# Cross-attention on one core: whole output tiles in sequence, the range check between the norms, and the choice loaded ahead of the wait for the stores

## The reference

```python
Q = (input_Q @ W_Q).reshape(b, -1, N_HEADS, D_K).transpose(0, 2, 1, 3)
K = (input_K @ W_K).reshape(b, -1, N_HEADS, D_K).transpose(0, 2, 1, 3)
V = (input_V @ W_V).reshape(b, -1, N_HEADS, D_V).transpose(0, 2, 1, 3)
scores = jnp.einsum('bhqd,bhkd->bhqk', Q, K) / np.sqrt(D_K)
attn = jax.nn.softmax(scores, axis=-1)
context = jnp.einsum('bhqk,bhkd->bhqd', attn, V)
context = context.transpose(0, 2, 1, 3).reshape(b, -1, N_HEADS * D_V)
out = context @ W_O + input_Q
mu = jnp.mean(out, axis=-1, keepdims=True)
var = jnp.var(out, axis=-1, keepdims=True)
return (out - mu) / jnp.sqrt(var + 1e-05)
```

## Time and profile before

| | before |
|---|---|
| median of 3 runs | 1643.43 us (1643.36 to 1644.0) |
| profiled execution, its own time | 1643.83 us |
| its span, first to last instruction | 1642.1 us |
| mean granted TensorE clock | 0.998 |
| TensorE matmul busy | 1626.4 us (99%) |
| VectorE busy | 1237.4 us (75%) |
| ScalarE busy | 964.8 us (59%) |
| GpSimd busy | 63.3 us (4%) |
| DMA, mean over the span | 6 GB/s |

### The profile page before, as it was taken

The page is one execution under the profiler, slowest core; times in us unless marked ns, Lnnn a source line. Parts: engine busy times, 40 slices in busy tenths (PEclk is TensorE's granted clock), DMA queues, the critical chain, the costliest instruction groups (busy, mean ns, idle before and its releaser), DMA issues.

```text
span 1642.1 us, 39623 instructions
## 1 busy us (share of the span) xinstructions
PE 1626.4 (99%) x17542; PEld 642.3 (39%) x17542; DVE 1237.4 (75%) x1184; ACT 964.8 (59%) x1079; POOL 63.3 (4%) x38
## 2 busy tenths in 40 slices
PE   9999999999999999999999999999999999999997
PEld 3443334333343334433344333443334433344334
DVE  5778787787877878777787777878777787777876
ACT  5556655555656556565655666556565565655652
POOL 0001010000100001000000100001000010000100
PEclk9999999999999999999999999999999999999999
DMA  4000000000000000000000000000000000000000
GB/s 158 2 2 1 2 2 2 1 1 2 1 2 2 1 2 2 2 2 1 2 2 2 2 1 2 2 1 2 1 1 2 2 2 1 2 2 2 1 1 15
DMA packets 6367, 9.53 MB, mean 6 GB/s; under 512 B 432, under 2 KB 4016, under 8 KB 6192
## 3 DMA queue, kind: packets, MB, share of 16 engines
q1 hardware_dynamic: 5760, 6.36, 1.2%
q10 hardware_dynamic: 432, 0.59, 0.1%
HBM read 6.42 MB, written 0.52 MB: 4 GB/s over the span
## 4 chain that ended last, share of the span: by engine, by line
PE 98%; DVE 1%; DMA 0%; ACT 0%; issue 0%; SPq 0%; ACTq 0%
PE o_ps L345 43%; PE s_ps L328 43%; PE w_ps L392 7%; PE w_ps L375 5%; PE s_ps L415 0%; DMA ctx_all<-in_ctxT 0%; PE o_ps L415 0%; PE w_ps L415 0%; ACT probs L509 0%; DVE sums L607 0%; DVE k_all L595 0%; DVE y L683 0%; DVE limits L619 0%; DVE y L666 0%; PE o_ps L392 0%
## 5 line engine op out<-in xcount | busy, mean ns | idle before, releaser
L607 DVE TENSOR_TENSOR sums<-sums,probs 128x1024 f32<-128x1024 f32 (+1 forms) x800 | 999.9, 1250 | 364.4 <-ACT probs L509 357.5
L509 ACT ACTIVATE probs<-s_ps 128x1024 f32<-128x1024 f32 x816 | 836.9, 1026 | 644.3 <-PE s_ps L328 626.6
L328 PE MATMUL s_ps<-q_sb,k_all 64*64 64x512 f32 x6528 | 846.8, 589 | 0.8 <-DVE q_sb L595 0.6
L345 PE MATMUL o_ps<-probs,v_all 64*64 64x512 f32 x6528 | 846.5, 589 | 0.0
L328 PEld LDWEIGHTS s_ps<-q_sb,k_all 64*64 64x64 f32 x6528 | 248.9, 133 | 452.2 <-issue 447.3
L345 PEld LDWEIGHTS o_ps<-probs,v_all 64*64 64x64 f32 x6528 | 244.7, 133 | 392.5 <-issue 388.0
L375 PEld LDWEIGHTS w_ps<-wv_sb,ctx_all 64*64 64x64 f32 x3232 | 96.3, 133 | 59.7 <-issue 52.0
L375 PE MATMUL w_ps<-wv_sb,ctx_all 64*64 64x128 f32 x3232 | 107.1, 270 | 0.4 <-DVE k_all L595 0.4
L392 PE MATMUL w_ps<-ctx_all,wk_sb 64*64 64x512 f32 (+1 forms) x832 | 106.9, 584 | 0.6 <-DMA ctx_all<-in_ctxT 0.6
L303 POOL TENSOR_TENSOR o_b<-o_a,o_b 128x512 f32<-128x512 f32 x15 | 31.5, 2098 | 1290.0 <-ACT o_a L540 1290.0
L595 DVE TENSOR_TENSOR k_all<-k_all,w_ps 128x512 f32<-128x512 f32 (+1 forms) x104 | 69.6, 669 | 6.6 <-ACT k_all L518 6.6
(11 more groups left out here) (52 smaller groups left out, 115.0 us busy)
## 6 DMA issues: line engine op xcount, KB each, us to landing
ctx_all<-in_ctxT SPq DMA_DIRECT2D x12, 256.0 KB, 5.6
xT_sb<-in_xT ACTq DMA_DIRECT2D x2, 256.0 KB, 4.5
x_sb<-in_x SPq DMA_DIRECT2D x1, 512.0 KB, 10.4
wo_sb<-in_wo SPq DMA_DIRECT2D x1, 512.0 KB, 11.4
out<-y SPq DMA_DIRECT2D x4, 128.0 KB, 2.0
wq_sb<-in_wq SPq DMA_DIRECT2D x1, 448.0 KB, 7.0
wk_sb<-in_wk SPq DMA_DIRECT2D x1, 448.0 KB, 7.7
wv_sb<-in_wv SPq DMA_DIRECT2D x1, 448.0 KB, 8.4
```

The source lines that it names most:

```text
L328: last = nc.tensor.matmul(s_ps[part(half), u % 2, head * QH:(head + 1) * QH], k_all[part(head), c * P + half * DH:c * P + (half + 1) * DH] ...
L345: last = nc.tensor.matmul(o_ps[part(head), rows, :], v_all[part(rows), c, part(head)], probs[part(rows), u % RING, head * QH:(head + 1) * QH],
L509: nc.scalar.activation(probs[:, u % RING, :], s_ps[:, u % 2, :], ACT.Exp, scale=SCALE).then_inc(probs_ready, 1)
L607: nc.vector.tensor_tensor(out=sums[0:rows, t % 2, :], in0=sums[0:rows, t % 2, :], in1=probs[0:rows, u % RING, :], op=ALU.add).then_inc(sum ...
```

## The change

TensorE projects tiles 4, 5, 6 and 7 whole, one after another. The wait for the last normalisation moves ahead of tile 4's eighth pair, and the counting matmul moves ahead of tile 7; it now waits for two tiles taken, where it waited for all eight. VectorE does the norm of tiles 0 to 3, then the range check with the choice, then the norm of tiles 4 to 7. SyncE loads the choice between the second and the third store. TensorE, ScalarE and VectorE load it where they did, at the end of their streams.

```diff
-        def if_general(eng, program):
+        def load_choice(eng):
             eng.wait_ge(choice_ready, 1)
-            chosen = eng.value_load(use_general[0:1, 0:1], min_val=0, max_val=1)
+            return eng.value_load(use_general[0:1, 0:1], min_val=0, max_val=1)
+
+        def if_general(eng, chosen, program):
             with eng.If(chosen > 0):
                 program()
...
-            def store(turn):
-                for n in range(QT // 2):
+            def store(turn, groups):
+                for n in groups:
                     sp.wait_ge(ln_done, QT * turn + 2 * n + 2)
                     sp.dma_start(out_t[:, 2 * n:2 * n + 2, :], y[:, 2 * n:2 * n + 2, :]).then_inc(stored, 16)
...
-            store(0)
+            store(0, (0, 1))
+            chosen = load_choice(sp)
+            store(0, (2, 3))
             sp.wait_ge(stored, 16 * (QT // 2))
-            if_general(sp, general_and_store)
+            if_general(sp, chosen, general_and_store)
...
             pe.wait_ge(o_added, PASSES)
-            for t in (4, 5):
-                project_output(t, range(PAIRS - 1))
+            project_output(4, range(PAIRS - 1))
+            pe.wait_ge(last_norm_done, 1)
+            project_output(4, [PAIRS - 1]).then_inc(y_done, 1)
+            project_output(5, range(PAIRS)).then_inc(y_done, 1)
 
             pe.wait_ge(work_ready, COUNT["d", PASSES - 1, 0])
-            for t in (6, 7):
-                project_output(t, range(PAIRS - 1))
-            pe.wait_ge(last_norm_done, 1)
-            for t in range(QT // 2, QT):
-                project_output(t, [PAIRS - 1]).then_inc(y_done, 1)
-
-
-            pe.wait_ge(y_taken, QT)
+            project_output(6, range(PAIRS)).then_inc(y_done, 1)
+
+            pe.wait_ge(y_taken, 2)
             pe.wait_ge(exact_ready, 1)
             nc.tensor.matmul(s_ps[0:1, 0, 0:1], exact[:, :], ones[:, 0:1], start=True, stop=True).then_inc(exact_counted, 1)
+            project_output(7, range(PAIRS)).then_inc(y_done, 1)
...
-            if_general(pe, general)
+            if_general(pe, load_choice(pe), general)
...
             dve.wait_ge(xres_loaded, 32)
-            layer_norm(0)
-
+            layer_norm(0, (0, 1))
 
             for n in range(2):
                 find_limit(last, n)
...
             nc.vector.tensor_scalar(out=use_general[:, :], in0=s_ps[0:1, 0, 0:1], scalar1=P - 0.5, scalar2=None,
                                     op0=ALU.is_lt).then_inc(choice_ready, 1)
 
+            layer_norm(0, (2, 3))
+
```

More of the change, by code:

```diff
@@ L280, in general_and_store @@
                 general()
-                store(1)
+                store(1, range(QT // 2))
                 sp.wait_ge(stored, 2 * 16 * (QT // 2))
             out_t = out.rearrange("(t p) d -> p t d", p=P)
-            store(0)
+            store(0, (0, 1))
+            chosen = load_choice(sp)
+            store(0, (2, 3))
             sp.wait_ge(stored, 16 * (QT // 2))
-            if_general(sp, general_and_store)
+            if_general(sp, chosen, general_and_store)
         @block.gpsimd
@@ L584, in _ @@
             roots(0)
-            if_general(act, general_and_roots)
+            if_general(act, load_choice(act), general_and_roots)
         @block.vector
@@ L656, in _, with layer_norm @@
                                     op=ALU.mult).then_inc(last_norm_done, 1)
-            def layer_norm(turn):
+            def layer_norm(turn, groups):
                 STEPS = 5
-                for n in range(QT // 2):
+                for n in groups:
                     before = STEPS * (QT // 2 * turn + n)
@@ L770, in general_and_norm @@
                 dve.wait_ge(stored, 16 * (QT // 2))
-                layer_norm(1)
-            if_general(dve, general_and_norm)
+                layer_norm(1, range(QT // 2))
+            if_general(dve, load_choice(dve), general_and_norm)
 def kernel(**inputs):
```

## The result

The changed kernel takes 1638.80 us (median of 9 runs, 1637.69 to 1639.22) against 1643.36 us (median of 9, 1642.35 to 1644.0): ratio 0.9973, 95% interval 0.9964 to 0.9982. It is faster, by 4.56 us, where 5.97 was forecast; the time lies 0.1 above the upper end of the range and 1.3 above the predicted one.

A forecast was written before the change was run, and what follows sets the result against it. TensorE's 4.18 us branch after the late choice bounds the kernel; afterwards SyncE's stores end it at 1635.9, plus 0.23: span 1636.13, 5.97 us saved. From the median 1643.43 that gives 1637.5 us, range 1636.7 to 1638.7.

The forecast's parts named there:

- What bounds the kernel before: At the kernel's end: choice at 1636.63, plus loading 0.87, TensorE's branch 4.18, DRAIN and barrier about 0.4 us.
- (1): TensorE doing tiles 4 to 7 in sequence: 1.79 us a tile, tile 6 whole at 1628.37, moved wait costs nothing.
- (2): Range check of 2.00 us fills VectorE's 3.58 us hole; TensorE's wait for it has 0.38 us slack, no cost.
- (3): Choice known at 1628.74 against 1636.63, 7.89 us earlier; VectorE idles from 1627.85 to 1628.74 for it.
- (4): Norms of tiles 4 to 7 on VectorE: last row of y ready at 1633.44, 0.76 us earlier.
- (5): SyncE's choice load hidden between stores 2 and 3, else 0.8 us; last store lands after 1.8 us; SyncE ends at 1635.9.
- rival B: TensorE's branch ends the kernel, its fetch falling among stores 3 and 4; 1638.4 us at 1.3 times its length; chance 0.09.
- (6): TensorE's branch stays and costs 4.18 us again but no longer starts last; through DRAIN at 1635.55, before SyncE.
- A: The stores end the kernel: 1637.5 us, own range 1636.7 to 1638.4; chance 0.82.
- C: Choice later than forecast, by a range check over 2.38 us or unhidden SyncE load; 1638.3 at 0.8 late; chance 0.04.
- D: SyncE's branch stalls behind the stores as TensorE's does; 1641.2 us, no measurable difference; chance 0.04.
- E: Slower: TensorE's branch needs its blocks one after another behind store packets; four stalls of 4.18 give 1649.7 us; chance 0.01.

The follow-up runs named there:

- the experiment: The changed kernel with SyncE's load of the choice put back behind the wait for the stores: 1639.42 us (ratio 0.9980).
- the rerun: The changed kernel itself measured once more, with no edit: 1638.49 us (ratio 0.9975), last store landing after 3.5 us.

## Why the prediction was right and where it was wrong

**What bounds the kernel before**: right, and shown by the kernel without TensorE's branch. Its span ended at 1638.5 and not at the 1638.0 that the text gave for a kernel with a short branch: VectorE's DRAIN at 1638.2 comes after SyncE's, and the 0.23 to the end of the span behind that.

**(1) and (2), TensorE's order and the check in the hole**: right. Tile 6 ends 12.71 us after the projection's start, as worked out, and TensorE never waits for the check: it ends at 1627.04, the counting matmul starts at 1627.55.

**(3), the choice**: 7.89 earlier forecast, 7.96 measured. VectorE waited 0.67 for it.

**(4), the last norms**: right within 0.2. The last store is issued at 17.60 after the start, forecast 17.79; the choice's end and the next norm's first addition overlap.

**(5), SyncE's queue**: the load is hidden, and its price of 0.8 is right (the experiment gave 0.9). The landing is the step that failed. I took 1.8 us, "the row of the store that, like this one, has a TensorE that is done". The rows had that wrong way round: what set the 2.6 us store apart was the packet of q8 in its time, which the earlier trace rows held and which the text used, under rival B, to argue that the stores would lengthen TensorE's branch. It was the other way: the branch's packets lengthen the store, here from 1.8 to 3.0 us. The text also moved TensorE's branch ahead by over 6 us without asking what else its fetch would meet, and it never placed the packets of ScalarE's and VectorE's jumps. The packet of TensorE that does the harm is the second one, behind the jump's end. In the kernel before it moved at 1642.4, after the end of the span, where the earlier trace rows did not look (the DMA view of 1642.1:1643.1):

```profile
q8 instruction: 1, 0.02, 6.0%
```

**(6), TensorE's branch**: right that it stays and is covered. It ran 1628.8 to 1632.2, the earlier of the two cases, and took 3.42 us where 4.18 was assumed; being covered, the difference moved nothing.

**The sum**: from the projection's start, 20.47 forecast and 21.35 measured in the first profile. The parts: issue 0.2 sooner, landing 1.2 later (3.0 for 1.8), SyncE's way from the landing to the end 0.13 shorter (0.75 for 0.88). In the rerun, whose profiled execution (1638.47) lies at its median, the landing is 1.7 later, and -0.2 + 1.7 - 0.1 = 1.4 from the projection's start. The medians miss 1637.46 by 1.3 (1638.80) and 1.0 (1638.49). The landing is thus the only part that is long enough for the miss; closer than that the account does not go, because the projection's start itself moves by up to 1.0 us from profile to profile.

**The range** allowed 0.8 for the landing, the worst row seen, which had one packet in its time. Here there were three. **The rivals**: A was right in kind, the stores end it. B, C, D and E did not come.

**How one packet does it** can be read in part. In the profile with q8 alone the packet ends 1.5 us after the issue, and the trickle begins there. In the rerun it starts at 0.9 and takes 1.5 us, so it ends at 2.4, and there the second part of the trickle begins. How many of the store's packets start more than 1.5 us after its issue is in the DMA view of the 2 us from there on, here with ScalarE's and VectorE's jumps held back (1634.05:1636.05), with TensorE's held back (1634.31:1636.31), and in the rerun (1633.82:1635.82):

```profile
q1 hardware_dynamic: 16, 0.01, 2.4%
```
```profile
q1 hardware_dynamic: 17, 0.01, 1.4%
```
```profile
q1 hardware_dynamic: 34, 0.02, 4.2%
```

In the kernel with no jumps on three engines there are none. 272 packets over 16 DMA engines are 17 each, so this looks like one engine that serves its share only behind the instruction packet, and two of them in the rerun. The other stores of the fourteen profiles say the same. The second always has a q8 packet in its data and lands after 2.3 to 2.8 us; the first always has one of q14 and lands after 2.0 to 2.3. In all, 17 stores meet a q8 packet alone while their data moves, and each lands 1.1 to 1.2 us after that packet's end. Stores whose packets all ended within 0.7 us of the issue, or started 1.46 us or more after it, land after 1.8 to 1.9. So what counts is less how many packets there are than when they end. No view shows the single engines, so that a packet and a share wait on the same one is inferred, not shown. How the packets lie in executions that were not profiled is open too.

## What to carry to other kernels

When a step is moved ahead, ask what its engines do next and where that now falls: a branch over a large untaken path fetches instructions, and a store whose landing ends the kernel should not share its time with such a fetch. Count the jump of every engine, not only of the slow one; holding the branches of finished engines back gave back 1.0 to 1.2 us here. Only a short jump (under 0.1 us on ScalarE and VectorE) may wait for the landing; TensorE's, of 3.4 to 4.2 us, had to start earlier, when its tiles were taken, and ended 0.2 us behind the landing (1635.0 and 1634.8 in the first such profile). Held until the landing it would have ended the kernel itself, by an estimate from these rows (1634.8 + 3.4 to 4.2, against the 1635.0 here) 3 to 4 us later; no run tried it. A branch whose price is 4 us wants its condition known early, even where the condition looks like bookkeeping at the end.

## What the runs showed of the hardware

The jump over TensorE's untaken path costs 3.42 to 4.18 us in the twelve profiles that have it, under 0.1 on the three other engines. It has two packets of q8: one 1.1 to 1.6 us after its start, and one 0.7 behind its end, 1.2 in the kernel with the tile order alone (1629.8 and 1632.9 in the changed kernel). The first takes 0.92 to 1.75 us, and the jump ends 1.4 to 1.5 us after it; so the jump scatters with this packet's start and length. The Trainium skill ("Runtime: NRT & Kernel Launch", section "Instruction fetch mechanics") says that a sequencer fetches the next block of instructions through a DMA queue of its own while it works on the one it has. The second packet of q8, after the jump's end, agrees with that. For the other engines the queue of their own does not show: the profile gives the packets of ScalarE, VectorE and SyncE one number, q14.

TensorE's sequencer is ahead of its matmuls: in the kernel without branches it reached its DRAIN at 1628.7 and stood there 1555 ns for tile 7.

```profile
L78 PEldq DRAIN  x1: 1555/1555/1555, 1628.7 to 1628.7; - x1
```

A 128 KB store whose data moves in about 0.5 us lands after 1.8 us undisturbed and after up to 3.5 us with three instruction packets of 0.01 to 0.02 MB in its time.
